# First experts in half blocks: expert slots dealt in units of 64, output product in two column groups

## The reference

```python
H = gelu(xf @ W1 + b1)                      # 3125 x 1024
probs = softmax(H @ Wg + bg)                # 8 experts
assign = argmax(probs)
for e in range(8):
    y = H @ Wd[e] + bd[e]                   # 1024 -> 256
    out += where(assign == e, probs[:, e:e+1] * y, 0)
```

## Time and profile before

| what | value |
|---|---|
| device time, median of 3 runs | 2574.71 us (2570.63 to 2580.15) |
| span of the profiled execution, first to last instruction | 2204.9 us |
| what lies around that span, by the median | 369.8 us |
| mean granted TensorE clock in it | 0.878 |
| busy share of PE, DVE, ACT, POOL | 80%, 58%, 40%, 53% |
| first experts, first output product to last store issued | 947.1 to 1101.9 us |

### The profile page before, as it was taken

One profiled execution on the slowest core, in us unless ns is written; L12 is line 12 of the kernel. 1 busy time (PEld: TensorE's weight loads), 2 busy tenths in 40 slices (PEclk: granted clock), 3 DMA queues, 4 the chain that ended last, 5 costly groups with the idle time before them and its releaser, 6 DMA issues. The chain is left out here.

```text
span 2204.9 us, 38514 instructions
## 1 busy us (share of the span) xinstructions
PE 1760.4 (80%) x11779; PEld 1497.5 (68%) x11780; DVE 1277.6 (58%) x2754; ACT 873.7 (40%) x1797; POOL 1173.9 (53%) x1179
## 2 busy tenths in 40 slices
PE   5737988878775899699708878878778699999996
PEld 4525766666654777588607767666657599999995
DVE  7337977777768633346667788877638722222221
ACT  4425765555553244322142222222225634333332
POOL 2667777777770400056567777777640045444442
PEclk9958987777887899899959898999978699999998
DMA  3588655555565362567567866666650566767775
GB/s 93 137 181 199 169 162 151 154 156 150 157 150 131 79 181 80 140 198 226 181 192 248 263 225 224 222 219 219 214 157 24 181 208 192 203 187 192 199 188 146
DMA packets 203516, 384.67 MB, mean 174 GB/s; under 512 B 43525, under 2 KB 138170, under 8 KB 203199
## 3 DMA queue, kind: packets, MB, share of 16 engines
q1 hardware_dynamic: 136871, 223.77, 33.5%
q0 software_dynamic: 65696, 157.37, 26.8%
q10 hardware_dynamic: 840, 2.16, 0.3%
HBM read 277.93 MB, written 108.69 MB: 175 GB/s over the span
## 5 line engine op out<-in xcount | busy, mean ns | idle before, releaser
L808 POOL DMA_INDIRECT qr<-q_rows,src_t x415 | 407.4, 982 | 126.5 <-issue 124.1
L2303 POOL DMA_INDIRECT fr<-pair_rows,dst_i x381 | 363.0, 953 | 123.6 <-issue 113.1
L2323 PE MATMUL psP<-f_part,onehot 125*128 125x256 bf16 x2925 | 359.8, 286 | 85.2 <-DVE onehot L2349 85.1
L2323 PEld LDWEIGHTS psP<-f_part,onehot 125*128 125x128 bf16 x2925 | 297.2, 103 | 141.2 <-DVE onehot L2349 95.1
L906 PE MATMUL psK<-kp,oh_k 126*128 x1680 | 281.5, 332 | 94.1 <-DVE qr L1011 66.1
L906 PEld LDWEIGHTS psK<-kp,oh_k 126*128 126x128 bf16 x1680 | 191.4, 115 | 164.8 <-issue 99.8
L2361 DVE SCALAR_TENSOR_TENSOR psA<-psA,same,fr 128x256 f32<-128x256 f32 x420 | 206.5, 492 | 75.0 <-DMA fr<-pair_rows,dst_i 42.9
L2443 ACT ACTIVATE acc<-psA 128x1280 f32<-128x1280 f32 x84 | 103.9, 1237 | 331.0 <-DVEq L2364 310.8
L1919 ACT ACTIVATE m1hT<-m1psH,m1par 128x128 f32<-128x128 f32 x448 | 127.7, 368 | 252.7 <-PE m1psH L1939 252.7
L1939 PEld LDWEIGHTS m1psH<-m1xT,n_rows 128*128 128x128 f32 x1792 | 208.7, 192 | 5.0 <-DMA n_rows<-in_L_ffn_W_dram 1.2
L1939 PE MATMUL m1psH<-m1xT,n_rows 128*128 128x128 f32 x1792 | 209.3, 275 | 1.7 <-DMA n_rows<-in_L_ffn_W_dram 1.1
(11 more groups left out here) (502 smaller groups left out, 2685.1 us busy)
## 6 DMA issues: line engine op xcount, KB each, us to landing
n_rows<-in_L_ffn_W_dram SPq DMA_DIRECT2D x56, 1024.0 KB
run_rows<-acc SPq DMA_DIRECT2D x84, 640.0 KB
loc<-locals_ SPq DMA_DIRECT2D x85, 157.5 KB
ea<-in_edge_attr_dram SPq DMA_DIRECT2D x84, 140.0 KB
w_first<-in_L_ffn_Wd_dram SPq DMA_DIRECT2D x8, 1024.0 KB, 11.8
w_all<-in_L_ffn_W_dram SPq DMA_DIRECT2D x8, 1024.0 KB, 10.3
m1b<-in_L_ffn_b_dram SPq DMA_DIRECT2D x56, 128.0 KB, 2.9
qr<-q_rows,src_t POOLq DMA_INDIRECT x420
```

The lines of the kernel that those rows point to most:

```text
L808: nc.gpsimd.indirect_dma_start(out=qr[:, n % GQ, u, :], out_offset=None, in_=q_rows, in_offset=bass.IndirectOffsetOnAxis(ap=src_t[:, n, u: ...
L2303: nc.gpsimd.indirect_dma_start(out=fr[:, n % GI, u, :], out_offset=None, in_=f_rows, in_offset=bass.IndirectOffsetOnAxis(ap=f_at[:, n * G ...
L2323: last = nc.tensor.matmul(psP[:, k % 2, 0:D], onehot[:, k % 2, t, :], f_part[:, c, t, :], start=(t == 0 and c == 0), stop=(t == T - 1 and ...
```

## The change

Slots are dealt in units of `U0` = 64. An expert gets as many units as it needs; two units that follow each other share a block of 128 slots, so a block may hold two experts. The constants become `NU0` = (3125 + 8 x 63) // 64 = 56 units and `NB0` = 28 blocks, 14 turns. `block_e` and `block_w` now have an entry per unit. `route` gets `unit` as an argument; the second routing passes `S` and stays as it was.

In the first experts each of the 8 slices becomes two products: the first 64 slots go to partitions 0 to 63 of `psY` with the first unit's weights out of `w2_first`, the last 64 to partitions 64 to 127 with the second unit's weights out of a new buffer `w2_half[s]`. ACT fills that buffer once per block, by one copy of 128 x 2048 out of `w2_first` at an address from a register. It stands behind the block's two `hT` copies, and the output product waits for it (`s_w2h`). Ahead of its loop ACT waits for all eight experts' weights. SP's bias load becomes two loads of 64 partitions.

```diff
-NB0 = (N_NODES + X * (S - 1)) // S
+U0 = 64
+NU0 = (N_NODES + X * (U0 - 1)) // U0
+NB0 = NU0 * U0 // S
...
-                step = sb(st, name + "step", [P, X, T])
-                full = sb(st, name + "full", [P, X, T])
+                step = sb(st, name + "step", [P, X, most])
+                full = sb(st, name + "full", [P, X, most])
...
-                b_of = sb(st, name + "b_of", [1, n_blocks, X])
+                b_of = sb(st, name + "b_of", [1, n_units, X])
...
-                    link(nc.vector.tensor_scalar(nblk[:, 0, :], nblk[:, 2, :], float(S), None, ALU.mult))
+                    link(nc.vector.tensor_scalar(nblk[:, 0, :], nblk[:, 2, :], float(unit), None, ALU.mult))
...
-        route("r0", 1, NB0, sems2, False)
+        route("r0", 1, NB0, U0, sems2, False)
...
+            w2_half = [n_rows[:].rearrange("p t d -> p (t d)")[:, n * KC * D:(n + 1) * KC * D].rearrange("p (k d) -> p k d", k=KC)
+                       for n in range(2)]
...
-                            e = sp.value_load(block_e[0:1, bass.ds(t * 2 + s, 1)], min_val=0, max_val=X - 1)
-                            sp.wait_ge(s_ye, t * 2 + s + 1)
-                            sp.dma_start(b2r[s][:], L0_ffn_bd[bass.ds(e, 1), :].to_broadcast([S, D])).then_inc(s_b2[s], 16)
+                            for h in range(UNITS):
+                                e = sp.value_load(block_e[0:1, bass.ds((t * 2 + s) * UNITS + h, 1)], min_val=0, max_val=X - 1)
+                                if h == 0:
+                                    sp.wait_ge(s_ye, t * 2 + s + 1)
+                                sp.dma_start(b2r[s][h * U0:(h + 1) * U0, :], L0_ffn_bd[bass.ds(e, 1), :].to_broadcast([U0, D]))\
+                                  .then_inc(s_b2[s], 16)
...
+                    act.wait_ge(s_w2f, 16 * X)
+                    act.sem_inc(s_y, 2)
                     with act.Fori(0, turns) as t:
                         for s in range(2):
+                            first = act.value_load(block_w[0:1, bass.ds(t * 4 + s * 2 + 1, 1)], min_val=0, max_val=(X - 1) * KC)
                             act.wait_ge(s_tr, t * 2 + s + 3)
...
                             last.then_inc(s_hT, 1)
+                            act.wait_ge(s_y, t * 2 + s + 1)
+                            nc.scalar.activation(w2_half[s], w2_first[:, bass.ds(first, KC), :], ACT.Copy).then_inc(s_w2h, 1)
...
                         pe.wait_ge(s_ye, b + 1)
+                        pe.wait_ge(s_w2h, b + 1)
                         for m in range(KC):
-                            last = nc.tensor.matmul(psY[:, s, 0:D], hT[s][:, m, :],
-                                                    w2_first[:, bass.ds(first + m, 1), :].rearrange("p a d -> p (a d)"),
+                            nc.tensor.matmul(psY[0:U0, s, 0:D], hT[s][:, m, 0:U0],
+                                             w2_first[:, bass.ds(first + m, 1), :].rearrange("p a d -> p (a d)"),
+                                             start=(m == 0), stop=(m == KC - 1))
+                            last = nc.tensor.matmul(psY[U0:S, s, 0:D], hT[s][:, m, U0:S], w2_half[s][:, m, :],
                                                     start=(m == 0), stop=(m == KC - 1))
```

More of the change, by code:

```diff
@@ L139, in build @@
         gate_i = sb(top, "gate_i", [S, NB1], I32)
-        block_e = sb(top, "block_e", [1, NB1], I32)
-        block_w = sb(top, "block_w", [1, NB1], I32)
+        block_e = sb(top, "block_e", [1, max(NB1, NU0)], I32)
+        block_w = sb(top, "block_w", [1, max(NB1, NU0)], I32)
         stats = sb(top, "stats", [P, G, 6])
@@ L1538, in build, with route @@
                   for n in range(2)]
-        def route(name, picks, n_blocks, done, ahead):
+        def route(name, picks, n_blocks, unit, done, ahead):
+            n_units, most = n_blocks * S // unit, -(-N_NODES // unit)
             s_pick, s_cum, s_onehot, s_map, s_iota, s_places, s_inblk, s_apart, s_onehot_act = (sem(name + n) for n in (
@@ L1586, in route @@
                 psM = ps(st, name + "psM", [128, 512])
-                b_of = sb(st, name + "b_of", [1, n_blocks, X])
-                be_f = sb(st, name + "be_f", [1, n_blocks])
+                b_of = sb(st, name + "b_of", [1, n_units, X])
+                be_f = sb(st, name + "be_f", [1, n_units])
                 psN = ps(st, name + "psN", [128, 512])
@@ L1627, in _ @@
                 def _(pool):
-                    nc.gpsimd.iota(step[:], pattern=[[0, X], [S, T]], base=0, channel_multiplier=0,
+                    nc.gpsimd.iota(step[:], pattern=[[0, X], [unit, most]], base=0, channel_multiplier=0,
                                    allow_small_or_imprecise_dtypes=True).then_inc(s_iota, 1)
-                    nc.gpsimd.iota(b_of[:], pattern=[[1, n_blocks], [0, X]], base=0, channel_multiplier=0,
+                    nc.gpsimd.iota(b_of[:], pattern=[[1, n_units], [0, X]], base=0, channel_multiplier=0,
                                    allow_small_or_imprecise_dtypes=True).then_inc(s_iota, 1)
@@ L1724, in _ @@
                     link(last)
-                    link(nc.vector.tensor_tensor(full[:], run[:, T - 1, :].unsqueeze(2).to_broadcast([P, X, T]), step[:], ALU.is_gt))
+                    link(nc.vector.tensor_tensor(full[:], run[:, T - 1, :].unsqueeze(2).to_broadcast([P, X, most]), step[:], ALU.is_gt))
                     link(nc.vector.tensor_reduce(nblk[:, 0, :], full[:], AX.X, ALU.add))
@@ L1757, in _ @@
                     link(nc.vector.tensor_tensor(b_of[:], b_of[:], nblk[0:1, 1, :].unsqueeze(1)
-                                                 .to_broadcast([1, n_blocks, X]), ALU.is_ge))
+                                                 .to_broadcast([1, n_units, X]), ALU.is_ge))
                     link(nc.vector.tensor_reduce(be_f[:], b_of[:], AX.X, ALU.add))
                     link(nc.vector.tensor_scalar(be_f[:], be_f[:], float(X - 1), None, ALU.min))
-                    link(nc.vector.tensor_copy(block_e[:, 0:n_blocks], be_f[:]))
-                    link(nc.vector.tensor_scalar(block_w[:, 0:n_blocks], be_f[:], float(KC), None, ALU.mult))
+                    link(nc.vector.tensor_copy(block_e[:, 0:n_units], be_f[:]))
+                    link(nc.vector.tensor_scalar(block_w[:, 0:n_units], be_f[:], float(KC), None, ALU.mult))
                     v.sem_inc(s_places, 1)
@@ L2083, in first_experts @@
             s_tr, s_hT, s_y, s_ye, s_yg = (sem("m0" + n) for n in ("_turned", "_hT_ready", "_y_done", "_y_ready", "_y_finished"))
+            s_w2h = sem("m0_half_w2_kept")
+            w2_half = [n_rows[:].rearrange("p t d -> p (t d)")[:, n * KC * D:(n + 1) * KC * D].rearrange("p (k d) -> p k d", k=KC)
+                       for n in range(2)]
             turns = n_blocks // 2
             assert n_blocks == 2 * turns and n_blocks % 4 == 0
+            UNITS = S // U0
             with ExitStack() as st:
@@ L2200, in _ @@
                     with pe.Fori(0, turns - 1) as t:
-                        first = experts_of(bass.ds(t * 2, 2))
+                        first = experts_of(bass.ds(t * 4, 4))
                         output(t, 0, first[0])
                         turn(t + 1, 0)
-                        output(t, 1, first[1])
+                        output(t, 1, first[2])
                         turn(t + 1, 1)
-                    first = experts_of(slice(n_blocks - 2, n_blocks))
+                    first = experts_of(slice(n_blocks * 2 - 4, n_blocks * 2))
                     output(turns - 1, 0, first[0])
-                    output(turns - 1, 1, first[1])
+                    output(turns - 1, 1, first[2])
                 @block.vector
@@ L2218, in finish_pair @@
                             rows = yr[:, q, 0:D]
-                            v.wait_ge(s_b2[s], 16 * (t + 1))
-                            v.wait_ge(s_y, b + 1)
+                            v.wait_ge(s_b2[s], 16 * UNITS * (t + 1))
+                            v.wait_ge(s_y, b + 3)
                             link(nc.vector.tensor_tensor(y_own[:, s], psY[:, s, 0:D], b2r[s][:], ALU.add))
@@ L2846, in _ @@
                 route_logits(4)
-        route("r1", 2, NB1, (), True)
+        route("r1", 2, NB1, S, (), True)
         experts("m1", NB1, tok1, s_tok[1], sum1, s_base[1], L1_ffn_W1, L1_ffn_W2, L1_ffn_b2, True)
```

## The result

The changed kernel takes 2559.83 us (median of 7 runs, 2554.31 to 2563.52), the kernel before 2572.68 us beside it (7 runs). The ratio is 0.993, with a 95% interval of 0.9906 to 0.9955. Each ratio is an estimate from all runs, with its interval, and not the quotient of the two medians: the medians are 12.9 us apart the first time (0.5%) and 18.6 us the second (0.8%). Together that is about 0.7% faster, 13 to 19 us. The forecast was 2563.1, 0.45% faster, with "within 0.5%" and "faster" at even chances.

The account below looks back on a forecast made before the run. PE and POOL were taken as nearly level. Thirty intervals of 4.61 us become 26 of 4.78 (-13.9), +1.8 start, +0.2 end, +0.3 routing: -11.6, from 2574.7 to 2563.1 us; range 2555 to 2576.

Parts of the forecast that it names:

- Fewer blocks: First experts' loop: 28 blocks for 32, four blocks worth 18.4 us at today's 4.61 us a block.
- The output product in two halves: First experts' output on PE: 32 half-width instructions overlap fully as 16 waves of 0.216 us, still 3.46 us a block.
- exposed weight loads: Rival, output product: loads can't run under the other half's stream, block 6.5 us, +36.6 us, 2611; chance 0.06.
- no overlap: Rival, output product: halves run one by one, 32 x 0.216 = 6.9 us, block 8.2 us, 2658; chance 0.05.
- Changing the width: PE, twice per block between full and half width: drains the pipeline, 0.40 us per block for entry, exit, load and lag.
- The block at 4.78: First experts' loop: PE's own block 4.73 us plus 0.05 for leftover waits; bounds 4.64 and 4.95.
- The start: First block has no cover for ACT's copy: PE starts at about 948.9 in place of 947.09, +1.8 us.
- The copy hidden: ACT's 1.95 us weight copy per block finishes before PE asks, with 1.5 us to spare, except in the first block.
- The end: Last two outputs follow each other with 0.2 us more for lag and entry; nothing changes from there to the last store.
- The sum: Whole kernel: -13.9 us for blocks, +1.8 start, +0.2 end, +0.3 routing, together -11.6 us.
- The rival with POOL's pace: POOL's store loop sets the pace, switches are free: block 4.64 us, -15.3 us, 2559.4; chance 0.26.
- What lies around the span: Time outside the traced span stays: span 2204.9 to 2193.3 us, so median 2574.7 to 2563.1.

Follow-up runs that it names:

- e7: The kernel before with four more blocks (36, all at full width): 2229.41 us, ratio 1.0101 to the kernel before.
- e1: The changed kernel's 28 blocks, output product at full width with the first unit's weights only, no ACT copy: 2549.77 us, ratio 0.9907 to the kernel before.
- e9: The changed kernel's 28 blocks at full width, first unit's weights only, no ACT copy, run once more: 2552.66 us, ratio 0.9911 to the kernel before.
- e5: The changed kernel with PE's work per block in four pieces, so four changes of width per block, not two: 2195.68 us, ratio 0.9935 to the kernel before.
- e2: The changed kernel with 64 units, so 32 blocks as before: 2580.82 us, ratio 1.0019 to the kernel before.
- e11: The changed kernel with one more copy of 128 x 1024 ahead of each block's weight copy: 2565.95 us, ratio 0.9948 to the kernel before.
- e6: The changed kernel with ACT's weight copy ahead of the block's two hT copies: 2186.6 us, ratio 0.9907 to the kernel before.
- e3: The changed kernel without ACT's weight copy and the wait on it, second unit's weights left out: 2552.13 us, ratio 0.9921 to the kernel before.

## Why the prediction came out as it did

- **Fewer blocks.** Right in kind, too small in size: priced at 4.61 a block (18.4 us for four), measured 19.9 to 22.9 where four are added (e7), and 22 to 25 of stage where four are taken away at the upper level (e1, e9). The price was the mean length, and left out that further blocks are longer than the mean and lengthen the tail (2.2 us in e7). POOL's stores wait 41.5 us for one another in e7, 34.0 in the first trace; that this is the cause is read from the traces and was not tested.
- **The output product in two halves.** Right: halves start together, 0.216 us from one wave to the next, as the gate products had promised. The two slow rivals, exposed weight loads and no overlap, are out; loads of 64 columns, 0.14 us each, run under a wave. The Trainium skill, "TensorE: Matmul & The Clock Gate", The mechanism, has a weight load overlap matmuls in flight only where the row group differs. The trace differs: both halves use all rows, and 16 waves follow each other at 0.216 us.
- **Changing the width.** The mechanism is right, shown by e5; its size was 0.40 and is 0.30. The Trainium skill, "TensorEngine Tiling (Array Packing)", Key Properties, says that a change of tiling mode drains TensorE. The trace agrees in kind, with 0.30 us for the pair. Term by term: the entry was priced at 0.09 and is 0.094, the load that nothing hides at 0.05 and is 0.051. The exit was taken from the gates (four column groups there, two here) at 0.21 and is 0.155, and the lag of the second half was added at 0.05 where the halves start, and end, 0.01 us apart.
- **The block at 4.78.** This is the step that failed, by its size. It took 0.10 too much for the switches (exit and lag) and added 0.05 for leftover waits that do not exist at the lower level: 4.63 in 25 of 26 intervals, close to the 4.6 that the prediction had named as a sign of being wrong. 26 x 0.15 = 3.9 us. In the same terms: 138.2 to 26 x 4.63 = 120.4 is -17.8, not -13.9.
- **The start.** Priced +1.8 with the first output. That is what the copy's 1.91 us (priced 1.95) gives. Not foreseen: PE idles 2.3 us there, the granted clock falls, and the first block takes 1.7 more. In every trace with a wait of over 2 us there (2.30, and in e2, e5 and e11 2.27, 2.25 and 3.14) the first block took 6.2 to 6.6 us; where it was 1.24 (the changed kernel at the upper level) or 0.39 (e6) the clock stayed and the block took 4.63.
- **The copy hidden.** Right at the lower level (PE waits for 1 of 28), nearly so at the upper (PE waits twice, 2.0 us; e3: 3.4 us of stage, 1.7 of which is the start).
- **Routing.** `full` and its sum take 0.57 and 0.56 us for 0.37 and 0.36, as priced; the stretch of the routing went from 24.5 to 24.7 us.
- **The end.** +0.2 foreseen. From block 26's output to the last store 16.2 us, 16.6 before: -0.4. The sum had no such term; why the tail is shorter no run shows.
- **The sum.** At the lower level -17.8 + 1.7 (slow first block) + 1.9 (start) - 0.4 = -14.6 for the stage, and the traces have 165.5 and 150.8. The forecast had -11.9 for it. At the upper level the stage goes from 173.5 to 159.3, -14.2, by other amounts: -13.1 in the loop (4.81 to 5.05 a block), +0.8 at the start, -1.9 in the tail. The times say 13 to 19 us, so what the other stages add is within their spread. That the forecast lies only 1.3 us from the difference of the first two medians (11.6 and 12.9) is luck. At the level that it was read from, its terms missed by 3.9 us in the blocks and 0.6 at the end, and by 1.7 the other way in the first block; at the level that was timed they came out otherwise again.
- **The rival with POOL's pace.** It gave the better number (2559.4) for the wrong reason: POOL did not set a pace of 4.64; the switches were cheaper, and PE, which never stands still, set 4.63. What was right in it, and in the prediction's remark that less than 0.3 us more per block is partly free, is that the block grew by only 0.02 us on the mean.
- **What lies around the span.** Wrong, and harmless only because the sum was a difference. A span 14% under the median should have told me that this trace was of an execution of another kind.

## What to carry to other kernels

Two products over half the array's columns, with different weights streaming, cost TensorE here what one at full width does (a wave every 0.216 us); each pair of changes between half and full width costs it 0.30 us, so batch the work of one width and count the pairs. What the kernel pays of that depends on how long TensorE waited before: the loop's blocks went from 4.61 to 4.63 us at one level and from 4.81 to 5.05 at the other. Before adding per-block work that precedes a product, look at the first block, which has no cover: the wait there also lost the clock, and moving the copy ahead of the other copies took both away. And compare the span of a trace with the time of its own execution before pricing anything from it.

## What the runs showed that was not expected

The same program runs at two levels, 2210 and 2570 us, fixed for all runs that were timed together. In the experiments the lower one came on chip 0 and the upper one on chips 3 and 12, one session each, so chip and session cannot be told apart. At the lower one ACT follows PE after 0.04 us wherever it is free, at the upper one in many blocks after 0.3 to 3.6 us, with the idle time often put down to "remote" or "issue" (the profile names no engine or DMA that ended the wait); the mean granted clock is 0.88 and 0.81. Ratios between kernels hold at both (0.993 and 0.9927 for the changed kernel). The cause is open, and no run here was made for it.
